# GpSimd masks, four weight rooms and an earlier output product in a fused four-layer kernel

## The chip, the cores and the metric

The kernel runs on one core of a Trainium2 chip, all batches and layers in one launch. The metric is the device time of that core in microseconds, the median of the runs.

## What is computed

Four layers act on a residual stream x of 4 batches, 1024 tokens and 512 features in float32; each reads a layer-normalised x and adds its output to it. Cut to what matters here:

```
x = x + attention(layernorm(x)); x = x + experts(layernorm(x))
x = x + ssd(layernorm(x));       x = x + experts(layernorm(x))

attention: kqv = x @ Wqkv + bqkv              # 16 heads of 32
  scores = einsum('bsnh,btnh->bnst', k, q) / sqrt(32)
  scores = triu(scores) - 10000 * tril(ones, -1); attn = softmax(scores, axis=2)
  out = einsum('bnkq,bknh->bqnh', attn, v); return out @ Wo + bo
ssd: proj = u @ W_in.T; xBC, z, A_log = split(proj)
  xBC = causal depthwise conv of 4 taps; x, B, C = split(xBC)    # 32 heads of 16, state 64
  M = (C B^T) * exp(segsum(-softplus(A_log))); y = M x + D x
  return y * silu(z + z_bias) @ W_out.T
experts: 8 experts of rank 16, the best 2 of them weighted by their softmax
```

## The kernel before

Every engine runs its own instruction list, and a semaphore per step (`Signal`, with `wait(engine, n, k)`) orders them. After a preamble that transposes W_in and W_out into DRAM (`in_t`, `wout_t`), a loop runs once per batch. TensorE's list is written out by hand, and work of several stages is interleaved in it. Most products take three matmuls (high by high, high by low, low by high parts): ScalarE casts the high part (`_hi`), GpSimd or VectorE subtracts to get the low part (`_lo`). Weights are loaded raw into the room where the low part will stand (`win_raw` and `win` are the same memory), the high part goes beside it.

**Attention.** Heads go in 8 pairs a batch: 4 groups g, two halves hf. The first pass (`group_scores_a`, L872 and L877) computes scores for the row maxima: nine groups of tiles per pair (MAX_GROUPS), each in the same PSUM banks, VectorE reduces them (`maximum`, L1675), and the next group waits for the reductions. The causal mask is added there by a bf16 matmul of the identity with `mask_ts`. The second pass has 12 units per pair (ORDER), each of 128 keys by up to 512 queries for two heads: `scores_b` (L915 and L919) computes scores less the maximum, ScalarE takes exponentials into `PR` (L1313, four buffers), and `weigh` (L934, L936) multiplies them with V and with ones. Eight of the 12 units lie on the diagonal (units 0 to 3 and 5 to 8); for those a bf16 matmul of the identity with `mask_st` (L915) puts -1e30 into the 128 leading columns of both heads before the scores are added. A pair runs in five sessions: maxima groups of the next pair, scores of two units, in hf 0 of groups 0 to 2 also one projection of the next group (`project`, 12 matmuls), another maxima group, and the weighing of two units (four in the last). The last pair of a batch has no next pair. GpSimd multiplies the outputs by the reciprocal sums (L1981), makes their low parts (`output_lo`, L1962), the low part of Wo (`wo_part`), of the projection weights (`group_lo`, L1920), and once a batch adds the output bias to the tokens (`residual`, L1951).

**z and x.** Eight products (t = 0 to 7, 24 matmuls each) of the SSD layer's z and x parts. The weights of t come from `in_t` through SP's queue (`xz_weights`), ScalarE casts them (`xz_hi`, L1366), GpSimd makes the low part (L1920). Even and odd t have one room each, so the load of t waits for product t-2. On SP's queue stand also the loads of `sg` from `grid_t` and the stores of the decay sums (`store_decays`, 16 issues), later read back by `pair_cums` and `pair_decay`.

**SSD pairs.** 16 pairs of heads: projections of pair n+1 are interleaved into pair n (`project_ahead`), with transposes of B (L1134), the state matmul (L1144), decay segments (L1111, exponentials L1428), C by B (`inner`, L1125), a GpSimd select for the causal mask (L2016), VectorE's product (L1789) and two output matmuls (L1163, L1171). The last pair has nothing to project. VectorE's convolution taps are L1777. The result y of a pair goes by four DMAs (L680) into `yt`, and after every fourth pair `gate_tile` (L1832 to L1839) makes the high and low part `gh`, `gl` of 128 channels.

**W_out's product.** `row_product` computes 8 tiles of 128 tokens over k = 0 to 3 (96 matmuls): three parts of four tiles first, then the fourth part when the last channels are gated, then tiles 4 to 7 whole. W_out is loaded into `wout_raw` during pair 14, cast by ScalarE after it (`wout_split`, L1256), and its low part `wol` is made by VectorE (L1850). `add_tiles` on VectorE adds each tile (L1529) and takes its statistics (L1479); after tile 5 it centres two tiles (L1505), and TensorE's next stage starts after the seventh addition with transposes (L766), then expert logits.

```
    for t in range(2, 2 * KT):
        xz_pe.wait(sp, b, t - 1)
        xz_weights(t)
```

## Time and profile before

| | us |
|---|---|
| median of 3 runs (lowest, highest) | 3099.93 (3096.14, 3100.57) |
| profiled execution, its own time | 3103.92 |
| its span | 3102.2 |
| TensorE matmul busy | 2868.8 (92%) |
| VectorE / ScalarE / GpSimd busy | 1941.5 / 1204.2 / 756.0 |
| mean granted TensorE clock | 0.979 |

The busy time of matmuls contains their pipelined ends, so back-to-back matmuls show as overlapping, and starts say more than durations. Times are counted from the start of the span. "Idle before" is the time that an engine stood still before an instruction, with what released it.

### The profile page before, as it was taken

To read this page: it belongs to the slowest core of one execution; us is meant where nothing else is said; L and a number is where in the kernel's file an instruction comes from. 1 tells how busy PE (TensorE), PEld (TensorE's weight loads), DVE (VectorE), ACT (ScalarE), POOL (GpSimd) and SP (SyncE) were. 2 spreads that over 40 slices of the span, in tenths; PEclk is the share of its full clock that TensorE was granted. 3 is DMA by queue.
4 is the path that set the end of the run, shared out by engine and by line. 5 is a ranking of instruction groups with operands and counts; after the bars stand their busy time and mean duration, and the time that the engine had idled before them with its cause. 6 is when DMAs were issued, how large, how long until landed. Compare 5 with 4: busy or idle time off the path is not lost.

```text
span 3102.2 us, 58883 instructions
## 1 busy us (share of the span) xinstructions
PE 2868.8 (92%) x20916; PEld 2084.0 (67%) x20916; DVE 1941.5 (63%) x2910; ACT 1204.2 (39%) x1913; POOL 756.0 (24%) x1045
## 2 busy tenths in 40 slices
PE   3899999999999999999989989999998999999998
PEld 3655577777665557777765547777776555777775
DVE  2555565777745563777665547477776555657777
ACT  2244334444135433444323452444421444344442
POOL 3301113333111111333311111233322011123331
PEclk7899999999999999999999999999999999999999
DMA  9323111111232202111133220211123230111112
GB/s 349 87 61 67 32 48 43 52 47 50 78 84 61 46 18 62 46 48 46 40 97 76 49 46 18 68 52 47 39 70 89 49 79 15 52 52 48 45 45 79
DMA packets 163781, 192.05 MB, mean 62 GB/s; under 512 B 43962, under 2 KB 103994, under 8 KB 161786
## 3 DMA queue, kind: packets, MB, share of 16 engines
q1 hardware_dynamic: 156126, 175.57, 20.8%
q10 hardware_dynamic: 7456, 13.90, 1.4%
q8 instruction: 116, 1.90, 0.3%
q14 instruction: 83, 0.68, 0.1%
HBM read 106.99 MB, written 23.36 MB: 42 GB/s over the span
## 4 chain that ended last, share of the span: by engine, by line
PE 69%; DVE 12%; issue 8%; DMA 3%; SPq 3%; ACT 2%; POOL 1%; ACTq 1%; DVEq 0%; POOLq 0%
PE ps L756 15%; PE ps L757 14%; PE ps L758 14%; PE ps L877 4%; DVE mneg L1675 4%; PE ps L1125 4%; PE ps L934 3%; PE ps L919 2%; PE ps L1111 2%; PE ps L872 2%; PE ps L1134 2%; PE ps L1171 2%; DMA win_raw<-in_t 1%; ACT PR L1313 1%; PE ps L766 1%
## 5 line engine op out<-in xcount | busy, mean ns | idle before, releaser
L756 PE MATMUL ps<-uh,win 128*128 128x512 f32 x1536 | 625.1, 407 | 17.2 <-POOL win L1920 16.5
L757 PE MATMUL ps<-ul,win 128*128 128x512 f32 x1536 | 602.7, 392 | 0.0
L758 PE MATMUL ps<-uh,win 128*128 128x512 f32 x1536 | 601.5, 392 | 0.0
L1675 DVE TENSOR_REDUCE mneg<-ps 128x1 f32<-128x896 f32 (+7 forms) x512 | 367.5, 753 | 361.7 <-PE ps L877 360.1
L1313 ACT ACTIVATE PR<-ps 128x1024 f32<-128x1024 f32 (+3 forms) x384 | 293.2, 807 | 317.4 <-PE ps L919 290.6
L756 PEld LDWEIGHTS ps<-uh,win 128*128 128x128 f32 x1536 | 289.6, 189 | 92.2 <-POOL win L1920 19.4
L758 PEld LDWEIGHTS ps<-uh,win 128*128 128x128 f32 x1536 | 289.4, 188 | 64.8
L2016 POOL TENSOR_SCALAR_AFFINE_SELECT LM<-LM 128x512 f32<-128x512 f32 x256 | 208.9, 827 | 492.4 <-ACT LM L1428 492.4
L757 PEld LDWEIGHTS ps<-ul,win 128*128 128x128 f32 x1536 | 290.3, 189 | 53.6
L1789 DVE TENSOR_TENSOR LM<-ps,LM 128x512 f32<-128x512 f32 x256 | 170.3, 686 | 242.8 <-PE ps L1125 198.5
L934 PE MATMUL ps<-PR,V 128*32 128x512 f32 (+3 forms) x1536 | 282.4, 492 | 5.0 <-ACT OT L1323 2.7
L936 PE MATMUL ps<-PR,ones 128*32 128x512 f32 (+3 forms) x1536 | 282.3, 492 | 0.0
L1777 DVE SCALAR_TENSOR_TENSOR Ct<-ps,cpt,Ct 128x1023 f32<-128x1023 f32 (+2 forms) x192 | 245.6, 1279 | 14.4 <-ACT Ct L1418 9.9
L1777 DVE SCALAR_TENSOR_TENSOR Bt<-ps,cpt,Bt 128x1023 f32<-128x1023 f32 (+2 forms) x192 | 243.7, 1269 | 1.9 <-ACT Bt L1418 1.6
L1920 POOL TENSOR_TENSOR win<-win_raw,win 128x512 fp32r<-128x512 f32 (+1 forms) x49 | 82.1, 1679 | 616.7 <-ACT win L1250 332.4
L1224 ACT CAST uh<-ps 128x512 fp32r<-128x512 f32 x128 | 73.6, 587 | 373.3 <-PE ps L766 373.3
L877 PE MATMUL ps<-KS,QS 96*128 96x512 f32 (+3 forms) x768 | 213.4, 377 | 0.0
L1428 ACT ACTIVATE LM<-ps 128x512 f32<-128x512 f32 x256 | 147.5, 601 | 124.2 <-PE ps L1111 124.1
L919 PE MATMUL ps<-QS,KS 97*128 97x512 f32 (+3 forms) x768 | 189.8, 364 | 1.4 <-ACT PR L1313 1.4
L934 PEld LDWEIGHTS ps<-PR,V 128*32 128x32 f32 x1536 | 79.0, 109 | 141.9 <-issue 92.9
L1687 DVE RECIPROCAL xh<-xh 128x128 f32<-128x128 f32 x128 | 116.1, 931 | 79.9 <-ACT OT L1323 79.9
L1418 ACT ACTIVATE Ct<-ps,cpt 128x1024 f32<-128x1024 f32 x64 | 77.2, 1207 | 207.7 <-PE ps L758 207.7
(228 smaller groups left out, 5150.8 us busy)
## 6 DMA issues: line engine op xcount, KB each, us to landing
raw<-in_t SPq DMA_DIRECT2D x128, 256.0 KB, 2.8
QS<-EV SPq DMA_DIRECT2D x192, 128.0 KB, 2.5
KS<-EV SPq DMA_DIRECT2D x168, 128.0 KB, 2.6
in_t<-tiles ACTq DMA_DIRECT2D x10, 1024.0 KB, 9.6
XN<-in_L_attn_a_x_dram SPq DMA_DIRECT2D x40, 256.0 KB, 5.2
win_raw<-in_L_attn_a_Wqkv_dram SPq DMA_DIRECT2D x34, 256.0 KB, 3.3
win_raw<-in_t SPq DMA_DIRECT2D x32, 256.0 KB, 2.8
edec<-ed_t SPq DMA_DIRECT2D x512, 16.0 KB, 1.6
```

The costliest lines, as they stand in the source:

```text
L756: pe.matmul(dst, hi_l, hi_r, start=first, stop=False)
L757: pe.matmul(dst, hi_l, lo_r, start=False, stop=False)
L758: return pe.matmul(dst, lo_l, hi_r, start=False, stop=last)
L877: i = pe.matmul(flat[:, off + c:off + c + m], QS[0:STACK, home(pair, hh), t * P:(t + 1) * P], KS[0:STACK, home(pair, hh), c:c + m], start= ...
L919: i = pe.matmul(ps[:, score_bank(u) + hh, 0:n], KS[:, home(pair, hh), s * P:(s + 1) * P], QS[:, home(pair, hh), t0:t0 + n], start=s * P < ...
L934: pe.matmul(ps[o:o + HS, 6, at:at + n], V[:, s, h:h + HS], PR[:, u % 4, hh, 0:n], start=(s == 0), stop=last)
L936: i = pe.matmul(ps[r:r + HS, 6, at:at + n], ones[:, 0:HS], PR[:, u % 4, hh, 0:n], start=(s == 0), stop=last)
L1313: act.activation(PR[:, u % 4, :, 0:n], ps[:, score_bank(u):score_bank(u) + 2, 0:n], ACT.Exp, scale=SCALE).then_inc(ex.sem, 1)
L1675: dve.tensor_reduce(mneg[:, hh, t:t + 1], flat[:, off:off + (t + 1) * P], AX.X, ALU.max, negate=True).then_inc(a_max.sem, 1)
L1777: dve.scalar_tensor_tensor(dst[:, par, k:L], wide(2 * w)[:, 0:L - k], cpt[:, par, w, at:at + 1], dst[:, par, k:L], ALU.mult, ALU.add).then ...
L1789: dve.tensor_tensor(LM[:, q, :], ps[:, 5 + q % 2, :], LM[:, q, :], ALU.mult).then_inc(m_dve.sem, 1)
L2016: pool.affine_select(out=v, in_=v, compare_op=ALU.is_ge, fill=0.0, base=0, pattern=[[0, 4], [1, P]], channel_multiplier=-1).then_inc(sel_p ...
```

## The change

The second attention pass loses its mask matmuls; instead GpSimd clears the part above the diagonal in the exponentials (`clear`), and the weighing of a diagonal unit waits for that. GpSimd's other work of the attention is placed between these selects, and `residual` comes ahead of the second group's low part. In MAX_GROUPS the smaller tile of a group stands first. z and x weights get four rooms. W_out is loaded somewhat earlier, cast inside pair 14, its low part made half by VectorE and half by GpSimd; 9 matmuls for each of tiles 0 to 3 are issued inside the last pair, for tiles 4 to 7 right behind it, and the fourth parts last, with eight banks in use. The last channels are gated in two halves, and two of the last four y stores are issued by ScalarE.

```diff
-MAX_GROUPS = [[(0, 7, 0)], [(0, 6, 0), (0, 0, 896)], [(0, 5, 0), (0, 1, 768)], [(0, 4, 0), (0, 2, 640)], [(0, 3, 0), (1, 3, 512)],
+MAX_GROUPS = [[(0, 7, 0)], [(0, 0, 896), (0, 6, 0)], [(0, 1, 768), (0, 5, 0)], [(0, 2, 640), (0, 4, 0)], [(0, 3, 0), (1, 3, 512)],
...
                     def xz_weights(t):
-                        sp.dma_start(win_raw[:, t % 2, 0, 1].rearrange("p k n -> p (k n)"), in_dram[r]).then_inc(s_xz[t % 2], 16)
+                        sp.dma_start(win_raw[:, t % 2, t // 2 % 2, 1].rearrange("p k n -> p (k n)"), in_dram[r]).then_inc(s_xz[t % 2], 16)
...
                     xz_weights(0)
+                    xz_weights(2)
                     w_pe.wait(sp, b * 2, TT)
                     xz_weights(1)
+                    xz_weights(3)
...
-                    for t in range(2, 2 * KT):
-                        xz_pe.wait(sp, b, t - 1)
+                    for t in range(KT, 2 * KT):
+                        xz_pe.wait(sp, b, t - 3)
+                        if t >= 6:
+                            sp.sem_inc(s_tick, 1)
+                            xzw_hi.wait(sp, b, t - 1)
                         xz_weights(t)
-                        if t == 2:
+                        if t == 4:
...
-                        if t == 4:
+                        if t == 6:
                             store_decays()
-                        if t == 6:
+                        if t == 7:
...
...
+                                if last and q == 1:
+                                    bc_pe.wait(sp, b * PAIRS + j + 1, 2)
+                                    sp.dma_start(wout_raw, wout_dram.rearrange("p (k n) -> p k n", k=KT)).then_inc(s_wout, 16)
...
                         ex.wait(pe, p, max(u - 1, 0))
-                        if s * P >= c * HB:
-                            for hh in range(2):
-                                pe.matmul(ps[:, score_bank(u) + hh, 0:P], identb[:, :], mask_st[:, :], start=True, stop=False, skip_group_check=True)
...
-                    ex.wait(pe, p, u + 1)
+                    if u in DIAGONAL:
+                        cleared.wait(pe, p, DIAGONAL.index(u) + 1)
+                    else:
+                        ex.wait(pe, p, u + 1)
...
+                    def fill(t):
+                        if ahead is None:
+                            if t == 0:
+                                gate.wait(pe, b, KT - 1)
+                                for i in range(2):
+                                    wout_lo[i].wait(pe, b, 1)
+                            if t == 2:
+                                bc_dve.wait(pe, n, 2)
+                            product_start(t)
...
                     segment(0)
                     project_ahead(0, 1)
+                    fill(0)
...
                     i.then_inc(ds_pe.sem, 1)
+                    fill(1)
                     inner(0)
                     segment(1)
...
                     project_ahead(1, 0)
+                    fill(2)
                     segment(2)
                     segment(3)
                     inner(1)
                     project_ahead(1, 1)
+                    fill(3)
...
+                for t in (5, 6, 4, 7):
+                    if t == 4:
+                        y_dve.wait(pe, b * PAIRS + PAIRS - 1, 1)
+                    product_start(t)
+                for t in range(TT):
+                    if t % HALF == 0:
+                        gate.wait(pe, b, KT + t // HALF)
+                    product_part(t, KT - 1).then_inc(w_pe.sem, 1)
+                w_add.wait(pe, b * 2 + 1, 1)
+                keep_awake(0, 10)
+                w_add.wait(pe, b * 2 + 1, TT - 2)
...
                     if later is not None:
                         pair_hi(n + 2, par, later)
+                    elif ahead:
+                        wout_split()
...
+                def clear(p, units):
+
+                    for u in units:
+                        until(ex, p, u + 1)
+                        v = PR[:, u % 4, :, 0:P]
+                        pool.affine_select(out=v, in_=v, compare_op=ALU.is_ge, fill=0.0, base=0,
+                                           pattern=[[0, 2], [1, P]], channel_multiplier=-1).then_inc(cleared.sem, 1)
+
+                residual()
                 group_lo(b * 4 + 1)
                 until(qkw_lo, b * 4 + 1, 1)
-                residual()
...
                 for g in range(GROUPS):
+                    p = b * 8 + g * 2
+                    clear(p, DIAGONAL[:4])
+                    if g > 0:
+                        scale(g - 1, 0)
+                    clear(p, DIAGONAL[4:])
+                    if g > 0:
+                        output_lo(g - 1, 0)
+                        scale(g - 1, 1)
+                    clear(p + 1, DIAGONAL[:2])
+                    if g > 0:
+                        output_lo(g - 1, 1)
                     if g == 2:
                         until(wo_hi, b, 1)
-                        for k in range(KT):
-                            wo_part(k)
+                        wo_part(0)
+                        wo_part(1)
+                    clear(p + 1, DIAGONAL[2:4])
+                    if g == 2:
+                        wo_part(2)
+                    clear(p + 1, DIAGONAL[4:])
```

## Rows read from the trace of the kernel before

**Rows 1.** The page: a busy row, and the chain that ended last by engine.
```profile
PE 2868.8 (92%) x20916; PEld 2084.0 (67%) x20916; DVE 1941.5 (63%) x2910; ACT 1204.2 (39%) x1913; POOL 756.0 (24%) x1045
...
PE 69%; DVE 12%; issue 8%; DMA 3%; SPq 3%; ACT 2%; POOL 1%; ACTq 1%; DVEq 0%; POOLq 0%
```

**Rows 2.** Timeline of TensorE in the attention: start, us, engine, line, operation, tiles, count.
```profile
955.20 0.29 PE L915 MATMUL ps<-mask_st,identb 128*128 128x128 bf16 x2
955.29 0.71 PE L919 MATMUL ps<-QS,KS 97*128 97x512 f32 x2
...
974.83 0.63 PE L919 MATMUL ps<-QS,KS 97*128 97x512 f32 x2
...
987.48 0.29 PE L872 MATMUL ps<-mask_ts,identb 128*128 128x128 bf16 x2 [0.57 <-DVE mneg L1675]
```

**Rows 3.** Waits in the second batch's attention: us in total, times, longest.
```profile
PE ps L872 <- DVE mneg L1675: 11.6, 41, 0.8
PE ps L915 <- ACT PR L1313: 3.6, 9, 0.9
```

**Rows 4.** Timeline of VectorE: two reductions of one maxima group each.
```profile
903.72 1.29 DVE L1675 TENSOR_REDUCE mneg<-ps 128x1 f32<-128x512 f32 x2 [0.24 <-PE ps L877]
...
983.93 1.29 DVE L1675 TENSOR_REDUCE mneg<-ps 128x1 f32<-128x896 f32 x2 [0.90 <-PE ps L877]
```

**Rows 5.** Timeline in an SSD pair: an exponential and the select behind it.
```profile
765.67 0.62 ACT L1428 ACTIVATE LM<-ps 128x512 f32<-128x512 f32 x1
...
766.46 0.63 POOL L2016 TENSOR_SCALAR_AFFINE_SELECT LM<-LM 128x512 f32<-128x512 f32 x1 [1.85 <-ACT LM L1428]
```

**Rows 6.** Timeline of a pair without projection: exponentials 0 and 1, weighing.
```profile
981.05 1.30 ACT L1313 ACTIVATE PR<-ps 128x1024 f32<-128x1024 f32 x2 [2.39 <-PE ps L919]
...
983.83 0.62 PE L934 MATMUL ps<-PR,V 128*32 128x512 f32 x1
```

**Rows 7.** The page's groups: busy, mean ns, idle before and releaser.
```profile
L756 PE MATMUL ps<-uh,win 128*128 128x512 f32 x1536 | 625.1, 407 | 17.2 <-POOL win L1920 16.5
```

**Rows 8.** The chain in order of time, second batch's z and x: start, us.
```profile
1190.90 9.56 DMA win_raw<-in_t
```

**Rows 9.** Windows, first batch's last SSD pair: us, busy by engine, clock, DMA.
```profile
763.90:777.50 13.60, 8.42 (x111) 5.96 (x111) 9.41 (x10) 7.22 (x14) 7.12 (x11) 0.94 0.28 89
```

**Rows 10.** TensorE's waits in that window, the first and last of seven.
```profile
PE ps L1125 <- DVE Ct L1777: 1.3, 1, 1.3
...
PE ps L1111 <- ACT LM L1428: 0.5, 1, 0.5
```

**Rows 11.** Timeline of TensorE: last pair's transposes, product's start, next stage.
```profile
763.99 1.06 PE L1134 MATMUL ps<-ident,Bt 128*128 128x128 f32 x8 [0.70 <-DVE y L1814]
...
777.45 0.80 PE L756 MATMUL ps<-woh,gh 128*128 128x512 f32 x1
...
801.13 1.03 PE L766 MATMUL ps<-ident,xh 128*128 128x128 f32 x8
...
803.26 0.39 PE L756 MATMUL ps<-wdr,uh 128*128 128x256 f32 x1 [1.10 <-DVE ul L1496]
```

**Rows 12.** Timeline of VectorE in the last stage: first and seventh addition.
```profile
3089.32 1.28 DVE L1529 TENSOR_TENSOR X<-ps,X 128x512 f32<-128x512 f32 x2
...
3097.63 0.69 DVE L1529 TENSOR_TENSOR X<-ps,X 128x512 f32<-128x512 f32 x1
```

**Rows 13.** Timeline: centring with and without GpSimd's additions, and the residual.
```profile
76.36 3.03 DVE L1505 TENSOR_SCALAR xh<-XN,mv,rstd 128x512 f32<-128x512 f32 x2 [0.60 <-POOL rstd L1916]
76.43 2.67 POOL L1920 TENSOR_TENSOR wv<-wv_raw,wv 128x512 fp32r<-128x512 f32 x2
...
848.01 0.54 DVE L1505 TENSOR_SCALAR xh<-XN,mv,rstd 128x512 f32<-128x512 f32 x1
848.61 0.66 PE L766 MATMUL ps<-ident,xh 128*128 128x128 f32 x4 [0.80 <-DVE xh L1505]
...
882.67 9.98 POOL L1951 TENSOR_TENSOR X<-XN,bob 128x512 f32<-128x512 f32 x8 [0.34 <-POOL win L1920]
```

More of the change, by code:

```diff
@@ L1377, in _ @@
                 act.activation(a_abs[:, :, :], a_abs[:, :, :], ACT.Ln, bias=1.0).then_inc(sp_act.sem, 1)
+                for t in range(2, KT):
+                    xz_hi(t)
                 def wide(bank):
@@ L2044, in _ @@
                                 taps_of(n + 1, j + 1, 1 - par)
-                            mix(n, j, par)
+                            if last and par:
+                                until(wout_hi, b, 1)
+                            mix(n, j, par, last and par)
                 value_lo(b + 1)
```

116 lines of the change are left out of this document (64 added, 52 removed).

## The prediction

> **What bounds the kernel now.** I read the profile's page first, then the chain of waits, then the waits by stage, and last single instructions in time. TensorE is busy for 92% of the span, and the chain that ended last runs over it for 69%, over VectorE for 12% [rows 1]. So work taken off TensorE should show, unless TensorE only waits longer for something else, and each edit has to be read in its own stage. The profiled execution took 3103.92 us around a span of 3102.2; the median of the runs is 3099.93, 4.0 lower. I make the sum on the profiled execution and carry it over unchanged. A measurement of this kernel can tell about 0.2%, 6.2 us.
>
> **Masks of the second attention pass.** Removed are 512 bf16 matmuls of 128 columns (L915): 8 diagonal units, 2 heads, 8 pairs, 4 batches. What one pair of them costs is read from starts: the first score matmul starts 0.09 to 0.10 us after the masks' first row, and two 512-column score matmuls then take 0.71 us where without masks in front two take 0.63 [rows 2]. The 0.08 is the load of the keys, which cannot hide behind a short mask. So a unit's two masks cost 0.18 us where TensorE flows, two units masked in one go 4 x 0.053 + 0.08 = 0.29, and after a wait, where the keys' load is exposed with or without a mask, I take 0.08. A head pair in full: units 0 and 1 0.29, units 2 and 3 0.16, unit 5 0.18, units 6 and 7 0.29, unit 8 0.18, together 1.10 us.
> It is not all on the path. In pairs with a projection inside the sessions (hf 0 of groups 0 to 2, 12 in all) VectorE has time, and all 1.10 counts: 13.2 us. In the other 20, TensorE waits for the maxima of the next pair, as in the row with 0.57 us of idle time [rows 2]; there are 41 such waits, 11.6 us in one batch, and 3.6 us for exponentials [rows 3]. A mask that goes only makes this wait longer. There, and in the last pair, where ScalarE sets the pace, only units 0 to 3 count, since the exponentials of the next session wait for them: 20 x 0.45 = 9.0. **Term: -22**; bounds 0, and 32 x 1.10 = 35.
> The Trainium skill (TensorE: Matmul & The Clock Gate, section "Wait — 56ns, not 53.3ns?") puts a warm 128-column bf16 matmul at 55.6 ns start to start; by that alone an estimate for all 512 is 28.5 us.
>
> **Selects in their place.** 256 GpSimd selects of 128x256 are added, and the weighing of a diagonal unit now waits for one. The trace has no such select; the nearest row is 0.63 us for 128x512, begun 0.17 us after its exponential ended at 765.67 + 0.62 [rows 5]; the lower bound is half of that. I take 0.4 behind a 0.17. The tightest place is a pair without projection: exponentials 0 and 1 end at 981.05 + 1.30 = 982.35 and the weighing of unit 0 starts at 983.83, of unit 1 0.4 later [rows 6]. Even 0.17 + 0.63 fits into 1.5. Elsewhere there are 3 us and more. Queued behind the selects on GpSimd are the scaling and the low parts of the attention output (about 1.3 us each), whose readers come a session later. In group 2 one low part and two pieces of Wo's low part stand ahead of unit 2's select, some 3.8 us, which I put 0.3 us late, once a batch. **Term: 0 to +1, taken as 0**.
>
> **Small maxima first.** Both orders reduce 1024 columns, and a pair of reductions takes 1.29 us for 896+128 as for 512+512 [rows 4]. TensorE waits for the whole group in either order. Weight loads that come behind a 128-column tile move from one group to another. **Term: 0**, bounds +-3.
>
> **z and x weights.** Before, room t is refilled only when product t-2 has ended, so load, ScalarE's cast and GpSimd's low part must fit into one product of 5.5 us. They often don't: a load behind the two grid loads took 9.56 us [rows 8], and TensorE waited 16.5 us for these low parts in four batches (the profile names them "win", and the waits lie in this stage alone) [rows 7]. With four rooms weights 2 and 3 are cast before product 0, and the load of 4 has three products, 16 us, to arrive. SP's queue moves with it: store_decays still follows product 2, and weight 7 now stands behind its 16 issues (9 us), ready about 8 us before product 7. The first pair's sums follow at once. The next stall would be x's transposes behind VectorE's taps, 0.2 us each. **Term: -16.5**; bounds -8 (if half come back behind other transfers) and -19.
>
> **W_out in the last pair.** Per batch, the last SSD pair lasts 13.6 us at a granted clock of 0.94 [rows 9], with seven waits of TensorE from 1.3 down to 0.5 us, 5.9 in all [rows 10]; it projects nothing. The change puts 36 product matmuls there. All 96 run from 777.45 to 801.13 with a 1.0 us wait, so 0.236 each, 36 are 8.5 us. The pair's own work is 7 to 7.7 us, so with 8.5 more TensorE fills it: 15.5 us, 1.9 longer, and less idle time for the clock to fall in.
> Then come another 36 before the last channels are needed, and the y stores are split over two queues, the gating over two halves; first half ready some 6 us after the pair's end, TensorE needs it after 8.5. No wait there. From the pair's start: 15.5 + 8.5 + 0.7 for tile 0 + 0.2 = 24.8 us until VectorE's first addition. Now 24 matmuls finish eight tiles in 5.7 us, and VectorE becomes the bound: in the kernel's last stage the same run of additions and statistics, with nothing to wait for, takes 3097.63 - 3089.32 = 8.3 us to its seventh addition [rows 12], which the next stage waits for. That gives 24.8 + 8.3 + 0.7 = 33.8 until the transposes; before it was 801.13 - 763.99 = 37.1 [rows 11]. The first logits come after three more VectorE steps of 0.6 and the low part of 0.7, at 35.7, against 803.26 - 763.99 = 39.3 [rows 11]. Ten keep-awake matmuls (2.3 us) lie inside the wait. W_out's low part leaves VectorE's queue ahead of the last pair; ScalarE's cast of 1.9 us moves into pair 14, between copies and exponentials, where it had 2 us to spare, if the 1 MB load, issued 4 us earlier, has landed. **Term: 3.5 x 4 = -14**; bounds 0, and -30 (37.1 less 7 and 96 x 0.236, all waits gone).
>
> **The residual, moved.** residual() is 8 GpSimd additions, 9.98 us, now at 882.67 beside reductions from PSUM. It moves to right behind KS's memsets, about 846.4, beside the centring that TensorE already waits for (0.80 us at 848.61). A centring takes 0.54 us alone and 3.03 for two while GpSimd adds run beside it [rows 13], so 1.0 more each. Two of them lie ahead of the first projection and are exposed. **Term: +2.0 x 4 = +8**; bounds 0, and four centrings, +16. It frees nobody: the copy that waited for it comes later.
>
> **Sum.** -22 - 16.5 - 14 + 8 = -44.5. 3103.92 - 44.5 = 3059.4; as a median 3099.93 - 44.5 = **3055.4 us**.
>
> **Rivals.** (a) Masks for nothing: TensorE's waits for maxima and exponentials grow by what the masks leave, in all pairs; for this speak 15 us of such waits in a batch, against it the sessions with projection. 3077.4. (b) The tail for nothing: fills hold the last pair's chain, since TensorE works in order and four blocks of 2.1 us each stand before a link of it; 3069.4. (c) Cheaper all round: masks pay wherever they stood, or the centring escapes the residual; with masks at 28 to 35 and the rest as summed, 3042 to 3049, and without the residual's 8 us 3047. The Trainium skill's 55.6 ns belongs with it: 3049 if all 512 counted. (d) The other side: late selects. If units 0 and 1 of the 32 pairs wait 0.7 us each for GpSimd, that is 45 us, and all is gone; from there it is slower. It needs a select of 0.17 + 2 us in the 1.5 us of [rows 6], as VectorE's two-input instructions might cause; the maxima read PSUM, which speaks against it. At 0.9 us each 3113. (e) Everything gives half, and the residual costs 16: 3099.93 - 26 + 16, near 3090; with a little of (d) within 0.2%.
>
> **Chances.** Forecast (3048 to 3063) 0.47; (a) 0.12; (b) 0.14; (c) 0.16; (d) 0.04; (e) 0.07, half of it within 0.2%. The range takes in (a) to (c): 3040 to 3079. Faster by over 0.2% 0.92, within 0.2% 0.04, slower 0.04.
>
> **What would show it.** L915 gone, and 256 selects of 0.3 to 0.64 us on PR. TensorE's waits for maxima per batch up from 11.6 to about 14, waits for "PR" by GpSimd under 1 us. No wait for "win" in the z and x stage. In the tail 34 us from the last pair's transposes to the next stage's, and three waits for additions. Centrings of about 1.5 us beside the residual. Wrong would be: weighing that waits for GpSimd in every pair, a last pair over 17 us, or centrings of 0.54.

## The result and the profile after

The changed kernel takes 3064.08 us in the median (3057.86 to 3067.11), the kernel before, measured beside it, 3099.29. The ratio is 0.9884 with a 95% interval of 0.9869 to 0.99. Measured a second time it is 0.9879 (0.9861 to 0.9896). So the change makes the kernel 1.2% faster, about 36 us. The forecast was 3055.4, which is 9 us too low. The measured time lies inside the range of 3040 to 3079, but 1 us above the band of 3048 to 3063 that the chances give to the forecast itself. The profiled execution took 3057.86 us and was the quickest of its four; a second trace of the same kernel has a span of 3063.3 us.

From the page of the changed kernel: busy times, the chain by engine, the group of the z and x products, and the new selects.

```profile
PE 2831.2 (93%) x20444; PEld 2054.0 (67%) x20444; DVE 1953.7 (64%) x2926; ACT 1202.4 (39%) x1913; POOL 869.8 (28%) x1305
...
PE 73%; DVE 14%; issue 5%; DMA 2%; ACT 2%; SPq 1%; POOL 1%; ACTq 1%; DVEq 0%; POOLq 0%
...
L765 PE MATMUL ps<-uh,win 128*128 128x512 f32 x1536 | 623.3, 406 | 0.6
...
L2008 POOL TENSOR_SCALAR_AFFINE_SELECT PR<-PR 128x256 f32<-128x256 f32 x256 | 101.9, 406 | 649.1 <-ACT PR L1352 649.1
```

Three steps can be read off at once. The idle time in front of the z and x products is 0.6 us where it was 17.2 [rows 7]. A select takes 0.406 us (I took 0.4). And the chain runs over TensorE for 73% in place of 69% [rows 1].

TensorE's waits in the attention of the second batch, in the changed kernel (total, times, longest):

```profile
PE ps L881 <- DVE mneg L1720: 13.9, 40, 0.8
PE ps L925 <- ACT PR L1352: 4.1, 10, 0.9
...
PE ps L925 <- DMA QS<-mrow: 1.5, 2, 0.8
```

The waits for the maxima rose from 11.6 us [rows 3] to 13.9; the forecast said about 14. No wait for a select appears: weighing never waits for GpSimd. The third row is new. It is a wait for the transfer that puts the row maxima into QS, and the forecast did not have it.

By stage, worked out from the starts of the first matmul of each stage, in the two traces and summed over the four batches (an SSD pair starts with its transposes of B):

| stage | before | after | change | forecast |
|---|---|---|---|---|
| attention, first maxima to its output product | 938.1 | 925.6 | -12.5 | -22 |
| z and x products to the first SSD pair | 229.3 | 206.8 | -22.5 | -16.5 |
| SSD pairs and W_out's product to the next logits | 1225.8 | 1214.1 | -11.7 | -14 |
| value product to the first maxima (residual) | 137.2 | 134.6 | -2.7 | +8 |
| those logits to the next batch's value product (three) | 105.6 | 107.7 | +2.1 | 0 |

**Where the z and x stage gained more than its waits.** In the kernel before, TensorE's timeline in the second batch has this, the first two product matmuls after a long wait and one 3 us later:

```profile
1202.59 0.79 PE L756 MATMUL ps<-uh,win 128*128 128x512 f32 x1 [3.66 <-POOL win L1920]
1203.18 0.63 PE L757 MATMUL ps<-ul,win 128*128 128x512 f32 x1
...
1205.74 0.47 PE L757 MATMUL ps<-ul,win 128*128 128x512 f32 x1
```

The same matmul takes 0.39 us elsewhere. The windows around it (us, busy by engine, granted clock, DMA) show why; the first is the kernel before, the whole stage and then the stretch behind the wait:

```profile
1190.70:1250.50 59.80, 53.78 (x273) 43.83 (x272) 22.64 (x20) 24.62 (x29) 12.26 (x18) 0.97 0.31 76
...
1202.50:1206.00 3.50, 3.42 (x8) 2.74 (x9) 0.00 (x0) 2.75 (x4) 0.60 (x2) 0.51 0.64 91
```

and this is the stage in the changed kernel:

```profile
1178.00:1229.70 51.70, 51.70 (x273) 42.68 (x272) 23.05 (x20) 23.86 (x28) 10.70 (x16) 1.00 0.29 74
```

Around the end of the wait of 3.66 us the granted clock fell to 0.51, the lower level of 1.2 GHz, for 3.4 us, and that cost another 1.5 us or so (eight distances of 0.31 to 0.59 us between starts in place of 0.23 to 0.34). Such a stretch stands in two of the four batches, behind this wait and behind one of 2.16 us; the waits of 2.36 and 2.67 us had none behind them. So the clock makes some 3 of the 6 us that the stages gained beyond their waits. The rest is about 0.3 us at each of the ten waits, also in the two batches without a slow stretch (3.4 and 5.0 us longer than after the change, with 2.6 and 4.2 us of waits): the last matmul in front of a wait, 0.27 us, runs out with nothing behind it and isn't counted as idle time. All four stages after the change last 51.7 us at 1.00, with TensorE busy throughout.

**The last SSD pair.** TensorE's timeline in the changed kernel: the pair's transposes, W_out's first matmul inside the pair, the next stage's transposes and logits.

```profile
757.28 1.06 PE L1162 MATMUL ps<-ident,Bt 128*128 128x128 f32 x8 [0.71 <-DVE y L1862]
...
758.42 0.39 PE L765 MATMUL ps<-woh,gh 128*128 128x512 f32 x1
...
790.32 1.11 PE L775 MATMUL ps<-ident,xh 128*128 128x128 f32 x8 [0.99 <-DVE xh L1550]
793.76 0.39 PE L765 MATMUL ps<-wdr,uh 128*128 128x256 f32 x1 [2.32 <-DVE ul L1541]
```

VectorE in the same stretch: first and seventh addition, and the low part that the logits wait for.

```profile
782.16 1.40 DVE L1574 TENSOR_TENSOR X<-ps,X 128x512 f32<-128x512 f32 x2 [0.49 <-PE ps L767]
...
790.63 0.69 DVE L1574 TENSOR_TENSOR X<-ps,X 128x512 f32<-128x512 f32 x1
...
793.02 0.68 DVE L1541 TENSOR_TENSOR ul<-ps,uh 128x512 fp32r<-128x512 f32 x1
```

From 757.28 the first addition comes after 24.9 us (forecast 24.8), the seventh 8.5 later (8.3), the transposes after 33.0 (33.8) and the logits after 36.5 (35.7). The transposes start 0.3 us ahead of the seventh addition: they wait for the centred tile (xh) behind the sixth, and not for the seventh, as the text ahead of the prediction and the forecast had it. The window of the pair shows TensorE filled, 15.52 of 15.60 us, at a clock of 1.00 where it was 0.94 [rows 9]:

```profile
757.20:772.80 15.60, 15.52 (x147) 11.95 (x147) 7.38 (x9) 6.27 (x13) 6.70 (x10) 1.00 0.24 77
```

**The residual beside the centring.** VectorE in the second batch, changed kernel, with GpSimd's residual from 837.32 for 10.73 us:

```profile
838.38 0.53 DVE L1550 TENSOR_SCALAR xh<-XN,mv,rstd 128x512 f32<-128x512 f32 x1
...
839.43 0.90 DVE L1550 TENSOR_SCALAR xh<-XN,mv,rstd 128x512 f32<-128x512 f32 x1
...
840.88 0.86 DVE L1550 TENSOR_SCALAR xh<-XN,mv,rstd 128x512 f32<-128x512 f32 x1
...
845.32 1.60 DVE L1550 TENSOR_SCALAR xh<-XN,mv,rstd 128x512 f32<-128x512 f32 x1
```

Alone a centring takes 0.54 us [rows 13]. Of these four one took 0.53, the others 0.86 to 1.60, and TensorE waited 0.99 and 0.76 us for two of them where it had waited 0.80 and 0.40. The forecast's 1.5 us was the worst case, not the usual one. VectorE's subtractions from PSUM between them (ul from ps and uh) kept their 0.68 us. The stage did not even grow, but that is no price of the residual: TensorE's wait for the transfer of KS at its end was 0.9, 0.9, 2.6 and 2.6 us in the four batches before and 0.9, 0.9, 1.9 and 1.0 after. Experiment 4 gives the price. The Trainium skill (GPSIMD Engine Reference, section "1. Specifications") says that GpSimd's SBUF interfaces are shared with VectorE, and that VectorE instructions contend in a 2-port mode or with two SBUF inputs; the longer centrings agree with that, if a centring runs in such a mode, which no run here shows.

### The profile page after: what moved, and what is told of

It reads as the page before. It is cut to its first block, busy times and chain, and to the rows that moved or that the text cites. A ratio compares the mean times of both kernels' runs of the same rounds, so it can differ in the third digit from the quotient of the medians.

```text
span 3056.1 us, 59013 instructions
## 1 busy us (share of the span) xinstructions
PE 2831.2 (93%) x20444; PEld 2054.0 (67%) x20444; DVE 1953.7 (64%) x2926; ACT 1202.4 (39%) x1913; POOL 869.8 (28%) x1305
## 4 chain that ended last, share of the span: by engine, by line
PE 73%; DVE 14%; issue 5%; DMA 2%; ACT 2%; SPq 1%; POOL 1%; ACTq 1%; DVEq 0%; POOLq 0%
PE ps L765 16%; PE ps L766 15%; PE ps L767 15%; DVE mneg L1720 6%; PE ps L886 4%; PE ps L1153 4%; PE ps L943 3%; PE ps L925 2%; PE ps L1139 2%; PE ps L1162 2%; PE ps L1203 2%; PE ps L881 2%; DVE X L1574 1%; ACT PR L1352 1%; PE ps L1173 1%
## 5 line engine op out<-in xcount | busy, mean ns | idle before, releaser
L1720 DVE TENSOR_REDUCE mneg<-ps 128x1 f32<-128x128 f32 (+7 forms) x512 | 367.5, 753 | 348.9 <-PE ps L886 347.5
L2008 POOL TENSOR_SCALAR_AFFINE_SELECT PR<-PR 128x256 f32<-128x256 f32 x256 | 101.9, 406 | 649.1 <-ACT PR L1352 649.1
L925 PE MATMUL ps<-QS,KS 97*128 97x512 f32 (+3 forms) x768 | 178.6, 354 | 21.4 <-ACT PR L1352 16.5
L925 PEld LDWEIGHTS ps<-QS,KS 97*128 97x128 f32 x768 | 126.9, 188 | 86.1 <-ACT PR L1352 37.1
```

Of the source, the lines that this page charges most:

```text
L925: i = pe.matmul(ps[:, score_bank(u) + hh, 0:n], KS[:, home(pair, hh), s * P:(s + 1) * P], QS[:, home(pair, hh), t0:t0 + n], start=True, st ...
L1720: dve.tensor_reduce(mneg[:, hh, t:t + 1], flat[:, off:off + (t + 1) * P], AX.X, ALU.max, negate=True).then_inc(a_max.sem, 1)
```

## The experiments

Each was timed against the kernel before. To read a term, I compare its ratio with 0.98815, the mean of the changed kernel's two; 0.001 is 3.1 us. Each ratio's interval is about 0.0013 to 0.002 wide on either side, 4 to 6 us, so the traces carry the smaller terms.

| run | median us | ratio | against the changed kernel |
|---|---|---|---|
| masks back as matmuls | 3073.48 | 0.9918 (0.9905 to 0.9932) | +11 us |
| residual at its old place | 3057.51 | 0.9870 (0.9853 to 0.9887) | -4 |
| two rooms for z and x | 3078.31 | 0.9937 (0.9920 to 0.9953) | +17 |
| W_out's product as before | 3069.78 | 0.9906 (0.9891 to 0.9922) | +8 |
| 32 increments ahead of TensorE's loop | 3072.26 | 0.9912 (0.9900 to 0.9925) | +9 |
| 64 increments | 3072.94 | 0.9911 (0.9897 to 0.9926) | +9 |
| larger tile first | 3064.55 | 0.9876 (0.9856 to 0.9896) | -2 |
| residual back and an earlier low part | 3057.34 | 0.9865 (0.9846 to 0.9884) | -5 |
| changed kernel again | 3064.79 | 0.9879 (0.9861 to 0.9896) | |
| chain of maxima first | 3072.76 | 0.9922 (0.9905 to 0.9938) | +13 |
| short maxima, one run | 2997.47 | | |
| short maxima with masks, one run | 2999.00 | | |

**1. Masks back.** GpSimd's other work stays in its new order; `clear` does nothing.

```diff
                         ex.wait(pe, p, max(u - 1, 0))
+                        if s * P >= c * HB:
+                            for hh in range(2):
+                                pe.matmul(ps[:, score_bank(u) + hh, 0:P], identb[:, :], mask_st[:, :], start=True, stop=False, skip_group_check=True)
...
-                    if u in DIAGONAL:
-                        cleared.wait(pe, p, DIAGONAL.index(u) + 1)
-                    else:
-                        ex.wait(pe, p, u + 1)
+                    ex.wait(pe, p, u + 1)
```

> The changed kernel, but with the mask matmuls of the second pass back and without GpSimd's selects. Forecast's term: 22 us slower than the changed kernel, with about 1.10 us more per head pair that has a projection in its sessions and 0.45 us more in each other pair. Reading of the two traces so far: the attention stage lost only 12.6 us in four batches, so 10 to 16 us slower; head pairs with a projection 1.0 to 1.1 us longer, the others about 0.2, since TensorE then waits less for VectorE's maxima. Rival: the trace of the changed kernel shows a new wait of TensorE for the transfer of the row maxima (QS from mrow), in pairs where a 16 KB instruction fetch starts 1 to 2.3 us after the maxima's transpose. If it is the fetch that makes it, its place depends on the count of TensorE's instructions, and with the masks back (and the selects away) the waits should vanish or appear in other pairs; if GpSimd's selects make it, it goes away in all pairs.

The attention took 937.4 us in four batches, 11.8 more than in the changed kernel, and the run was 11 us slower. A pair without projection, from one transpose of its maxima to the next, is 24.29 us long with the masks:

```profile
974.59 0.28 PE L911 MATMUL ps<-ident,mneg 128*16 128x128 f32 x1 [0.40 <-DVE mneg L1720]
...
998.88 0.28 PE L911 MATMUL ps<-ident,mneg 128*16 128x128 f32 x1 [0.39 <-DVE mneg L1720]
```

and 24.12 without them, in the changed kernel:

```profile
965.68 0.28 PE L911 MATMUL ps<-ident,mneg 128*16 128x128 f32 x1 [0.39 <-DVE mneg L1720]
...
989.80 0.28 PE L911 MATMUL ps<-ident,mneg 128*16 128x128 f32 x1 [0.39 <-DVE mneg L1720]
```

Pairs with a projection: 32.14 against 31.12, 33.90 against 32.81, 33.50 against 32.41. So the masks of a pair cost 1.0 to 1.1 us where there is a projection (forecast 1.10), 0.18 where there is none and 0.25 in the last pair of a batch, 21.69 against 21.44 (forecast 0.45 for both). No wait for the row maxima's transfer is left.

What holds the pairs without projection is seen in VectorE's timeline of the changed kernel:

```profile
973.17 1.29 DVE L1720 TENSOR_REDUCE mneg<-ps 128x1 f32<-128x128 f32 x2 [0.96 <-PE ps L886]
975.37 1.29 DVE L1720 TENSOR_REDUCE mneg<-ps 128x1 f32<-128x256 f32 x2 [0.91 <-PE ps L886]
977.55 1.29 DVE L1720 TENSOR_REDUCE mneg<-ps 128x1 f32<-128x384 f32 x2 [0.90 <-PE ps L886]
```

Neither engine is full: VectorE waits 0.9 us for TensorE's scores, TensorE up to 0.75 us for VectorE's reductions, and a group follows the other every 2.19 us, since all use the same banks. With masks the distance is 2.19 as well. Only what TensorE does ahead of the first group of a pair counts, and that is the masks of units 0 and 1 (the first reduction comes 5.5 us behind the transpose with them, 5.3 without). I had counted units 2 and 3 too.

**2. Short maxima, without and with masks.**

```diff
-                    dve.tensor_reduce(mneg[:, hh, t:t + 1], flat[:, off:off + (t + 1) * P], AX.X, ALU.max, negate=True).then_inc(a_max.sem, 1)
+                    dve.tensor_reduce(mneg[:, hh, t:t + 1], flat[:, off:off + min(t + 1, 2) * P], AX.X, ALU.max, negate=True).then_inc(a_max.sem, 1)
```

> The changed kernel, but each reduction of the row maxima reads at most the first 256 columns of its tile, so VectorE does less (the maxima are then those of a part of the row; the rest of the computation is as before). In the changed kernel a head pair without projection repeats every 2.19 us: scores of a group, two reductions of 1.29 us, scores of the next group in the same banks. Theory: this chain sets the pace there, not TensorE's work, and so a mask that goes only lengthens the wait. With reductions of about 0.8 us the pair falls from 24.1 us to between 20.5 and 22.5, and the mask's price shows in it (next run). Rival: TensorE's work sets the pace, and the pair stays within 0.5 us of 24.1.

> The same short reductions, with the mask matmuls back and the selects away. With full reductions the masks cost 0.18 us in a head pair without projection and 1.0 to 1.1 in one with it. Theory of the chain of maxima: with short reductions they cost 0.7 to 1.1 us in every pair. Rival (the masks are cheap there for another reason): still 0.2 us in the pairs without projection.

The first expectation held: the pair fell to 20.79 us, in this timeline of the kernel with short maxima:

```profile
945.65 0.27 PE L911 MATMUL ps<-ident,mneg 128*16 128x128 f32 x1
...
966.44 0.27 PE L911 MATMUL ps<-ident,mneg 128*16 128x128 f32 x1
```

The loop of scores and reductions did set the pace. The second missed. With masks the same pair took 21.29 us, so they cost 0.5 and not 0.7 to 1.1; in the seventh pair of a batch it was 0.34, and in the sixth the kernel with masks was quicker, 21.3 against 21.9. The 0.5 can be followed in VectorE's starts: the first reduction comes 0.2 us later with masks, the distance to the second is 0.2 longer and one behind it 0.1 longer. So units 2 and 3 count when the loop is quicker, and the rest still hides in its waits. In the sixth pair the selects became visible. TensorE's wait in that pair, short maxima, second batch:

```profile
PE ps L943 <- POOL PR L2008: 1.1, 1, 1.1
```

It is in group 2, where the pieces of Wo's low part stand ahead of a select, the place that the prediction named and priced at 0.3 us a batch. At the full pace of the maxima this lateness was hidden; in a kernel with 3 us less a pair it is not.

**3. The wait for the row maxima.** In the changed kernel eight transfers of the row maxima make TensorE wait, 0.3 to 1.0 us each and 4.7 in all, and each has a 16 KB instruction fetch that starts 1.0 to 2.3 us behind the transpose; in the kernel before no fetch falls there and TensorE never waits for one. DMA queues over the 3.9 us from such a transpose (share of 16 engines), a late case:

```profile
q1 hardware_dynamic: 147, 0.41, 47.9%
q8 instruction: 1, 0.02, 2.2%
q10 hardware_dynamic: 32, 0.01, 0.9%
```

and TensorE behind it:

```profile
1050.94 0.47 PE L925 MATMUL ps<-QS,KS 97*128 97x512 f32 x1 [0.78 <-DMA QS<-mrow]
```

The pair before it had twice the traffic, 95.8% of the engines' time on q1, but no fetch (q10 carries the maxima), and no wait:

```profile
q1 hardware_dynamic: 290, 0.80, 95.8%
q10 hardware_dynamic: 32, 0.01, 1.0%
```

Two runs moved the fetches by increments of an unused semaphore ahead of TensorE's loop:

```diff
+            for _ in range(32):
+                pe.sem_inc(s_tick, 1)
             with pe.Fori(0, NB) as b:
```

> The changed kernel with 32 semaphore increments on TensorE ahead of its loop over the batches; nothing else. They cost nothing inside a batch and move every later instruction of TensorE by 32 places. Theory: the waits for the row maxima come from a 16 KB instruction fetch on the same DMA engines, one for about 256 instructions of TensorE. In the changed kernel one falls 1.0 to 2.0 us after the maxima's transpose (23 and 31 matmuls and weight loads behind it) in the second and the seventh head pair of a batch. 32 places earlier none falls into the 3 us behind any transpose: no wait for QS from mrow, the second pair at 24.1 us and the seventh near 24.7 in all batches, up to 6 us faster in all. Rival, chance or the selects: the waits stay in the same pairs.

> As the run with 32 increments, but 64. Theory of the fetch: the second and seventh pair are free, but the third and the fifth pair, whose fetch stands about 105 places behind the transpose in the changed kernel, now have it about 41 places behind, some 2 to 3 us: waits move there, if the row maxima have not landed by then. Rival: the waits stay where they were, or vanish everywhere.

With 32 the second pair was free in all four batches, 24.10 to 24.12 us against 24.11 to 24.82. But the fifth pair now had a fetch at 1.5 to 1.8 us and waited in all four (32.8 to 33.15 against 32.4), and the seventh kept its own, which I had said would go. From the timeline with 32 increments, fifth pair:

```profile
1003.62 0.87 PE L927 MATMUL ps<-QS,KS 97*128 97x512 f32 x4 [0.70 <-DMA QS<-mrow]
```

With 64 the second pair was free too. The fifth had a fetch at 1.5 to 2.1 us and waited in all four batches, 0.3 to 0.8 us, as expected, and so did the seventh, which should have been free. The third had fetches in two batches; they fell on a transfer that lands at 3.1 us without a fetch too, and no wait came of it. So the waits go with the fetches, and their place with the count of instructions, but not by my rule of so many places: in the attention a fetch follows the last after 170 to 345 recorded instructions. In place of up to 6 us faster, both runs were 9 us slower. The first value product starts at 93.3 and 98.8 us, where it starts at 87.2 to 90.7 in the twelve other traces, so 5 and 10 us of delay come with the increments (in the traces they go out one by one, 0.15 us apart, up to 90.8 and 96.2 us); and with 32 the attention took 7 us more, the fifth and seventh pairs' waits above all.

Another transfer seems to be hit too. In the sixth pair of three batches with the masks back and of two in the kernel before, a fetch starts 0.7 to 0.9 us ahead of the transpose, TensorE waits 0.4 to 0.5 us for KS in front of the first maxima group, and the pair takes 24.9 us in place of 24.3. But three more sixth pairs of these two kernels have a fetch 0.6 to 0.8 us ahead and no such wait.

**4. Residual back.**

```diff
-                residual()
                 group_lo(b * 4 + 1)
                 until(qkw_lo, b * 4 + 1, 1)
+                residual()
```

> The changed kernel, but with the residual addition of GpSimd back behind the second group's low part. Forecast's term: 8 us faster, 2.0 in each batch, centrings at 0.54 us again in place of 0.8 to 1.6. Rival, from the two traces: of the stage from the value product to the first maxima, 137.3 us in four batches before and 134.6 after, nothing is lost, because the wait for the transfer of KS at its end (2.6 us before, 1.0 after) takes the delay up; then within 2 us. One batch of the changed kernel waited 1.9 us for a centring and ran at a granted clock of 0.89 in this stretch, 37.8 us in place of 32 to 33; if the residual beside the centrings causes that, no batch shows it now (4 us). Other rival: the residual, 10 us, now stands in front of the first pair's selects, and the weighing of unit 0 waits for GpSimd, 1 to 3 us a batch slower.

It was 4 us faster by the ratio, 6.6 by the medians; its interval and the changed kernel's overlap, but a second kernel with this edit (7, below) came out at the same 3057, and the stage says the same. From the value product to the first maxima, summed over four batches, it takes 133.6 to 140.4 us in the ten traces with the residual at its new place (their other edits lie outside this stage), 137.5 in the mean, and 131.5, 131.8 and 134.6 in the three with it back, 132.6 in the mean. So the residual costs some 5 us. The rival that the wait for KS takes the delay up did not come: this wait is 1.0 us with the residual back too. No weighing waited. One part of the 5 us is the two centrings: TensorE's waits for them are 1.2 us a batch with the residual back, and 1.2, 1.75, 2.7 and 2.2 in the changed kernel. The other part is the clock. In the run with the larger tile first, where the residual stands at its new place, this is the stretch behind the centrings that TensorE waited for:

```profile
846.40:849.80 3.40, 3.40 (x9) 2.67 (x9) 1.34 (x2) 0.58 (x1) 3.40 (x4) 0.51 0.00 0
```

and with the residual back the same part of the stage:

```profile
841.00:860.00 19.00, 18.15 (x86) 14.85 (x87) 8.54 (x14) 5.15 (x9) 0.00 (x0) 1.00 0.10 22
```

Most batches of both kernels have a slow stretch 32 to 37 us behind the logits. A second one behind it came, in the second to fourth batches, in 17 of 30 of the ten traces with the residual at its new place, and in none of the nine of the three with it back. (First batches stand apart, they follow other work; one in ten and one in three have it.) That is also why one stage of the changed kernel lasted 37.8 us and the others 32 to 33. That the longer waits for the centrings bring the second stretch is argued from this count; no run sets the waits alone.

**5. Two rooms for the z and x weights.** All lines of the change that put `t // 2 % 2` as a room are undone, with the loads, casts and waits around them.

```diff
-                    for t in range(KT, 2 * KT):
-                        xz_pe.wait(sp, b, t - 3)
+                    for t in range(2, 2 * KT):
+                        xz_pe.wait(sp, b, t - 1)
```

> The changed kernel, but with two rooms for the z and x weights, as before the change. Forecast's term: 16.5 us slower, the waits for the low parts alone. Reading of the traces: 22.5 us slower, because after a wait of several us for a low part the granted clock falls (0.97 over the second batch's stage, 53.8 us of TensorE busy for the same matmuls that take 51.7 at 1.00), so some 6 us come on top of the waits. If the lower clock in the kernel before had another cause, the stage shows the waits and 51.7 us of busy time in each batch.

17 us slower, and the four stages took 56.7, 55.1, 54.8 and 54.7 us, 14.5 more than 51.7 each. TensorE's waits for win in the whole run, and below the first and the second batch's stage as windows:

```profile
PE ps L760 <- POOL win L1960: 9.9, 10, 1.9
```

```profile
440.50:497.20 56.70, 53.84 (x274) 43.90 (x273) 22.64 (x21) 24.51 (x29) 11.92 (x17) 0.97 0.29 76
1190.40:1245.50 55.10, 52.50 (x273) 42.76 (x272) 22.61 (x20) 24.59 (x29) 11.89 (x17) 1.00 0.30 78
```

So 9.9 us of waits cost 14.5. The slow clock came in one batch of four only, for 3.4 us, and made some 1.5 of the 4.6 us beyond the waits. The other 3 are again 0.3 us at each of ten waits: the second window is 3.4 us longer than 51.7, with 2.6 us of waits, at a clock of 1.00. The clock alone, as the expectation had it, is not enough. The waits were shorter than in the kernel before (16.5 us, the longest 3.7); why the loads were quicker here is open. That the timed 17 us stand so near the forecast's 16.5 is luck, since the waits that these 16.5 us counted were 9.9 here.

**6. W_out's product as before the change.** Undone are the fills, the order of the products, the split gating, `wol` in halves, the load's place and the y stores.

```diff
                     segment(0)
                     project_ahead(0, 1)
-                    fill(0)
...
+                wout_lo.wait(pe, b, 1)
+                row_product(lambda dst, k, t0, first, end:
```

> The changed kernel, but with the output product of the SSD layer behind the last pair, the gating in one piece, the load, cast and low part of W_out and the y stores as before. Forecast's term: 14 us slower, 3.5 a batch (35.7 against 39.3 us from the last pair's first transposes to the next stage's logits). Reading of the traces: 36.5 against 39.3, so 2.8 a batch and about 11 to 12 us in all; the granted clock over the last pair falls from 1.00 to between 0.84 and 0.94. If instead the fills hold the pair's chain, the pair without them takes over 2 us less than 13.6 us, and the difference is below 8 us.

From the last pair's transposes to the logits it took 40.7, 38.2, 39.8 and 40.7 us against 36.5, 3.4 a batch, near the forecast's 3.5. By the ratio only 8 of the 13.4 us are left. Some 2 to 3 are given back: from the logits to the next value product the changed kernel needs 35.7 to 36.2 us, this one 35.1 to 35.3, as the kernel before. The pair's window in the first batch shows what the fills also bought:

```profile
755.50:770.30 14.80, 11.53 (x111) 8.30 (x111) 9.46 (x10) 7.00 (x14) 7.19 (x11) 0.63 0.24 81
```

The clock in the last pair is 0.63, 1.00, 0.87 and 0.63 in the four batches (0.94, 0.84, 0.74 and 0.81 in the kernel before, 1.00 in all of the changed kernel). In the batch at 1.00 the fills are worth 1.7 us (38.2 against 36.5). The rest of the 13.4 us, about half, came in the three batches with a slow stretch.

**7. An earlier low part, and the order of the tiles.**

```diff
                 for t in range(TT):
+                    if t == TT - 1 and early:
+                        lo(stats_of, 0)
                     product.wait(dve, n, t + 1)
```

> The changed kernel with the residual addition back behind the second group's low part, and VectorE's low part of the first normalised tile (ul) made ahead of the eighth addition of the attention's and the SSD layer's output, in place of behind it and two statistics. In the changed kernel TensorE waits 2.3 us for this ul before the first logits. Theory: this wait falls to about 1.1 us, 1 us a batch or more in both layers, and with it the slow clock that begins at the logits in three of four batches; 5 to 9 us faster than with the residual's place alone. Rival: ScalarE's cast of the tile, which ul reads, ends later than assumed, VectorE waits for it in front of the eighth addition, and the next tile's statistics come later: no gain.

> The changed kernel with the larger tile first in each group of maxima, as before the change. Forecast's term: 0, bounds 3 us either way. The chain of maxima, 2.19 us a group, has the same columns in either order, so the pairs without projection stay at 24.1 us. Rival: the shorter tile in front lets VectorE begin sooner; then the larger first makes the period longer by up to 0.2 us a group, 1.4 us a pair in 20 pairs, and the run some 20 us slower.

> The changed kernel once more, beside the two others. Its ratio to the kernel before is expected within 0.9869 to 0.99, as measured. What differs between this trace and the first one shows how much of a stage's time is chance: the waits for the row maxima in the second and seventh head pair, and the stretch from the value product to the first maxima, 32 to 38 us with the granted clock.

The wait for ul fell from 2.32 to 1.13 us, as in this row of the kernel with the earlier low part:

```profile
795.38 0.39 PE L765 MATMUL ps<-wdr,uh 128*128 128x256 f32 x1 [1.13 <-DVE ul L1541]
```

From W_out's product to the logits of the SSD layer it is 34.1 us in place of 35.3, and nothing of that comes back later.

But in the attention layer the logits start only 0.1 us earlier, and the stage of the experts behind them takes 35.4 us in place of 34.2. There the rival came: VectorE waits 2.6 us for ScalarE's cast (uh) in front of the eighth addition. And in both layers TensorE now waits 1.3 us more for a centred tile (xh) right behind the logits. In the SSD layer this second loss is made up for: the slow stretch at the logits, which is there in four of six batches of the changed kernel's two traces and in all three of the one with the residual back, is gone in all three. So some 1.2 us a batch are won in one layer and lost in the other, and 3057.34 against 3057.51 us says the same. The edit in the SSD layer alone, worth some 5 us by these stages (an estimate, four times 1.2), wasn't tried.

The larger tile first made no difference, 24.09 to 24.13 us a pair, as the forecast had it. The changed kernel again waited for the row maxima in seven of its eight second and seventh pairs; its longest second pair, 26.32 us, has a wait of 1.1 us and a slow stretch of the clock in it.

**8. The chain of maxima first.** The base has the residual back.

```diff
-                            if ahead:
+                            if ahead and (k or pair == 0):
                                 group_scores_a(p + 1, pair + 1, FILLING[k][0])
...
                         if ahead:
+                            if pair + 2 < 2 * GROUPS:
+                                m_act.wait(pe, p + 1, 1)
+                                group_scores_a(p + 2, pair + 2, 0)
                             scores_b(p + 1, pair + 1, (0, 1))
```

> The changed kernel with the residual addition back behind the second group's low part, and, in six of the eight head pairs of a batch, the first group of maxima scores of the pair after next issued ahead of the next pair's scores of units 0 and 1, behind a wait for ScalarE's copy of the row maxima. Theory: in a pair without projection the chain of maxima (nine groups, 2.19 us each) sets the pace, and it begins 4.5 us behind the transpose, after the last weighing and behind the 0.74 us of those scores, which also wait for the transfer of the row maxima. With the chain begun first, such a pair falls from 24.1 to about 23.4 us, and the scores meet their row maxima 0.7 us later, so that waits for QS from mrow fall from 5 us to under 2: 10 to 18 us faster than with the residual's place alone. Rival: ScalarE becomes late in its place, since its exponentials of units 0 and 1 come 0.7 us later; TensorE then waits for the scores' banks and the weighing by as much, and nothing is gained. Other rival: in pairs with a projection TensorE's own work sets the pace, and only the pairs without gain, 5 to 8 us.

It lost 16 us against its base; a pair without projection takes 24.81 us. The waits of one such pair:

```profile
PE ps L881 <- DVE mneg L1723: 2.6, 7, 0.8
PE ps L925 <- ACT PR L1355: 0.9, 1, 0.9
...
PE ps L881 <- DMA KS<-EV: 0.4, 1, 0.4
```

The waits for the row maxima's transfer are gone, as expected, but the first rival happened, and more than it: the exponentials of units 0 and 1 start 5.5 us behind the transpose in place of 4.55, and the scores of the next session, queued in order ahead of the second maxima group, wait 0.9 us for ScalarE. In the whole run TensorE's waits for the exponentials are 30.4 us, 15.7 in the base. The third row was in nobody's account: the maxima group that was moved ahead reads KS, and now meets its transfer, 11.4 us of waits in the run where the base has 3.9. With 4.5 us of waits for the row maxima gone, that makes the 16. The chain of the maxima runs through TensorE's order, and so through ScalarE and the transfer of KS.

## Why the prediction was nearly right

The mechanisms were the ones forecast: masks pay beside a projection, the rooms end the waits for win, the fills make a pair of 15.5 us and VectorE the bound behind it, the selects hide. Rivals (b), (d) and (e) did not come; of (a), that waits grow by what the masks leave, nearly all is true in the pairs without a projection, and nothing in the others. The time itself lies between the forecast and (b), 8.7 us from one and 5.3 from the other, so it does not tell them apart; the stages do. Four sizes were off, and they partly cancel.

- **Masks, -22; measured -11 to -13.** The part beside projections, 13.2, is right: 12 pairs at 1.0 to 1.1. The step that failed is "units 0 to 3 count" in the other 20: only units 0 and 1 do, 0.18 a pair (0.25 in the last pairs) and 4 us in all, in place of 9.0. And the step that a wait only takes up what a mask leaves overlooked the transfer of the row maxima, which has to arrive meanwhile. Late ones cost roughly 5 us in the traced run: the second, fifth and seventh pairs summed are 6.3 us above 24.11, 32.41 and 24.7 us (the seventh's 24.9 before, less 0.2), and over 1 us of that is a slow stretch of the clock inside one of them; the waits themselves sum to 4.7.
- **z and x, -16.5; measured -22.5 in the traces, -17 timed.** I counted waits and left out what hangs on them: the granted clock behind two of them, some 3 us, and about 0.3 us at each of ten, another 3.
- **W_out, -14; measured -12 to -13 up to the logits, -8 timed.** The working held to within 0.8 us at each of its four points, in part by two errors that cancel. The 33.8 us stands for the end of the seventh addition, for which the transposes do not wait. And from there three steps of 0.6 us and the low part of 0.7 lead to 36.3 us, not to 35.7; measured are 36.5. Added up rightly the term is 3.0 a batch, -12, which is what the two traces show. Left out was what comes behind: 0.7 us a batch in the next stage. There a slow stretch of the clock lies inside it in each of the three batches, where in the kernel before it began at most 1.3 us ahead of the stage's end. The wait of 2.3 us ahead of the logits is the likely reason where the stretch begins at the logits: with the wait at 1.1 us, in experiment 7 and with the tail as before, no batch has one there.
- **Residual, +8; measured +4 to +7, 5 by the stage.** The size is about right, the mechanism half: TensorE's waits for two centrings grew by 0, 0.55, 1.5 and 1.0 us in the four batches, 3 us in all, not by 2.0 each batch. The rest fits the second slow stretch, in 17 of 30 batches against none of nine.
- **Order of tiles, 0; measured -2 with an interval of 6.** Right.

The sum of -44.5 was carried from one execution to the median. The traced run of the changed kernel made -46.1, the medians -35.9. So the sum agrees with the traces by luck: the z and x stages gave 6 us more and the stage of the residual 11 us more than forecast, the masks 9 us less, and the changed kernel's trace was the quickest of its runs, the one before slower than its median. Two traces of one kernel differ by 7 us through late transfers and slow stretches, and I had no allowance for it. The four terms as timed one by one, 11, 17, 8 and -4, add up to 32 us of the 36.

Open: why the fetch delays the small transfer, when the heavy traffic of the stacks does not.

## What to carry to other kernels

A wait of TensorE is priced with what hangs on it. Read the granted clock of the stretch behind, since it can be low there, but in each batch: here it was low behind some waits and not behind others of the same length. Compare also the stage's length with the sum of its waits, since each wait cost some 0.3 us beyond what is counted as idle. A wait that is gone gives all of it back. Where two engines wait for each other in turn over the same banks, neither shows as full, and removing work from one gains only what stands outside that loop; look at the distance between repeats, not at the busy share. And when a step ahead of a transfer's reader is shortened or moved, ask how long the transfer needs and what else moves on its engines, instruction fetches too. A sum that comes out right is to be compared with the stages all the same.

## What was not expected of the hardware

With a fetch of 16 KB on the instruction queue behind the transpose, a transfer of 8 KB landed 3.2 to 4.0 us behind it in place of 2.2 or 2.5, while 0.80 MB of other traffic in 3.9 us left it at 2.5 to 2.6. Where a fetch falls changes with the count of instructions on the engine, so edits far away move it: 32 increments took it out of the second pair and put it into the fifth. Increments of a semaphore ahead of the loop were not free: the first value product came 5 us later with 32 of them and 10 us with 64, some 0.15 us each.
